# The seven late batches of x in L1's attention: rounded on a seven-step schedule, in place, and read back from DRAM

## The chip, the cores and the metric

The kernel runs on one core of one Trainium2 chip. The metric is the device time of one execution in microseconds. The core's engines are TensorE (PE, with its weight loads as PEld), VectorE (DVE), ScalarE (ACT), GpSimd (POOL) and SyncE (SP), which here only issues DMAs.

## The reference

The model takes x of 16 batches x 128 tokens x 256 and a context of the same shape through four layers, each `x = x + tanh(g) * attention(layernorm(x), ctx)` and then `x = x + tanh(g) * ffn(layernorm(x))`. The change lies in the attention of layer 1 (`_L1_xattn_ref`), cut to what matters:

```python
def _div_clamp_fp8(x, scale):
    y = jnp.clip(x / scale, -448, 448)
    y = y.astype(bfloat16)
    return fp8_e4m3_roundtrip(y)

ln_out = _ln(hidden_states, ln_w, ln_b)
q  = lin(ln_out, wq,  q_in_scale)     # each lin: _div_clamp_fp8(ln_out, its scale), then a matmul
k  = lin(ln_out, wk,  k_in_scale)
v  = lin(ln_out, wv,  v_in_scale)
qx = lin(ln_out, wqx, qx_in_scale)
q, k, qx = _ln per head (128 wide)
core = _gqa(q, k, v)                  # 16 heads, 8 groups
xout = _gqa(qx, _ln(kx), vx)          # kx, vx from the context, not rounded
catq = _div_clamp_fp8(concat(core, xout), proj_smooth)
return einsum(catq, wproj)
```

So the layer-normed x of each batch is needed in four versions, each scaled by its own vector and rounded to fp8. The rounding is done in bf16 with five operations on DVE (`round_fp8`).

## The kernel before, in words

Layer 1's attention (`l1_attention`) takes the 16 batches twice, once for each half of the eight head groups: Q = 32 passes q, each of J = 4 head groups, so N = 128 units n = 4q + j. Odd j are the cross-attention halves (they project the context too, L1525). The work is a software pipeline over steps s = 0 .. N + 21, which every engine walks through in the same order, each doing its own part of units at different depths:

- PE, in a step: `project(s-13)` (L1519, opens the step; the cross units L1525 too), `turn_x` for a late batch, `score(s-16)` (L1534), `values(s-18)` (L1543), `out_project(s-20)` (L1556), `turn_heads(s-15)` (L1567) and last `turn_probs(s-17)` (L1575), which waits for POOL's normalised probabilities.
- POOL, in a step: `statistics(s-14)` (L1832 to L1842: six small operations, of which the first waits for DVE's sum of squares L1756), the probabilities (L1876), the rounded output `l_cat` (L1883), then for a late batch `affine` (L1851, two operations), and in every step with s % 4 == 1 `put_cx_low` (L1858). All of it stands in one queue, in that order.
- DVE, in a step: smooth (L1736), sum of squares (L1756), the norm of the heads (L1767, both inputs in SBUF), row sums, maximum (L1778), five roundings of the output, and for s % 4 == 0 the addition to x (L1789).
- ACT, in a step: exponent (L1609), copies from PSUM (L1616, L1623), squares (L1630), the conversion of rounded x to fp32r for the matmuls (`put_xq`, L1665, `l_xq<-l_xs`), heads (L1637, L1638).

The rounded, four-fold x of a batch is 128 x 1024 bf16 (256 KB). For the batches 0 to 8 (AHEAD = 9) it is made earlier, beside the MoE layer of L0, and stored in DRAM (`saved`). The batches 9 to 15, called late, are made in the pipeline itself, during the first 16 passes: batch b in the steps from 4b on. Counted from s = 4b: +1 DVE normalises x (`norm_x`, L1772); +2 PE transposes it (`turn_x`) and ACT copies it out (`put_xb`); +3 ACT makes version 0 and POOL version 2 (`affine`); +4 ACT version 1, POOL version 3; +5, +6, +7, +7, +8 DVE does the parts 0, 1, 2, 3, 4 of `round_fp8` (L1244, L1246, L1248, L1250, L1251). Part 4 writes `XS` (`l_xs`), from which ACT reads one step later; SP also stores it to `saved` for the second 16 passes. SP fetches `XS` from DRAM for the other passes, at s = 4q + 5 for pass q, four steps before `put_xq` reads it.

The order of all work is written out by hand in the functions `sync`, `tensor`, `scalar`, `vector` and `gpsimd`; engines wait for each other through semaphores, and each engine runs its queue in order.

## Time and profile before

| what | value |
|---|---|
| median of 3 runs | 2357.87 us (2356.43 to 2365.08) |
| profiled execution, its own time | 2360.09 us |
| its span, first to last instruction | 2358.3 us |
| PE busy | 2120.3 us, 90% |
| DVE busy | 1872.0 us, 79% |
| ACT busy | 1358.7 us, 58% |
| POOL busy | 1246.9 us, 53% |
| mean granted TensorE clock | 0.956 |
| DMA | 82.35 MB, 10.1% of 16 engines' time in the main queue |

The span is shorter than the execution's own time by 1.8 us, which lies before the first and after the last instruction. The steps of L1's attention run from about 444 to 1260 us. In the views that follow, a row of a timeline is one instruction or a run of equal ones on one engine: its start from the span's start, its length, and in brackets how long the engine had been idle and who ended that. A busy POOL or DVE instruction may include time in which it was held up after it had started: the same operation on the same shape then shows two lengths.

### The profile page before, as it was taken

The numbers are of one execution on the slowest core, as the hardware profiler recorded it, in microseconds if no ns is written. First come the engines' busy times: TensorE is split into PE (matmuls) and PEld (weight loads), VectorE is DVE, ScalarE is ACT, GpSimd is POOL, SyncE is SP. The second block draws the span as 40 slices with busy tenths as digits, with TensorE's granted clock in tenths as the row PEclk, the third lists the DMA queues.
The fourth block names the chain that finished last, engine by engine and source line by source line (L and its number), as shares of the span: only waits on it lengthen the run. The fifth ranks groups of instructions, "written<-read, shape, count | busy, mean of one in ns | idle before, by whom it ended". The sixth has DMA issues, their size and how long they took to land.

```text
span 2358.3 us, 42828 instructions
## 1 busy us (share of the span) xinstructions
PE 2120.3 (90%) x14158; PEld 1760.8 (75%) x14158; DVE 1872.0 (79%) x3851; ACT 1358.7 (58%) x3426; POOL 1246.9 (53%) x1752
## 2 busy tenths in 40 slices
PE   5969999699999988999997899998899998659997
PEld 2348888589888877888886788886788887336665
DVE  5865687699999988999998677776578886777886
ACT  2213354688888877888885433333354455767773
POOL 4913343288999978999996211110344454741222
PEclk9979999799999999999999999998799999878998
DMA  4211121310000020000000300001000000010001
GB/s 133 83 38 65 43 86 54 125 35 18 11 17 15 23 81 19 17 15 19 17 6 13 119 21 27 21 21 59 8 8 8 8 6 1 1 50 20 24 24 37
DMA packets 39930, 82.35 MB, mean 35 GB/s; under 512 B 6048, under 2 KB 25824, under 8 KB 35776
## 3 DMA queue, kind: packets, MB, share of 16 engines
q1 hardware_dynamic: 39712, 79.60, 10.1%
q8 instruction: 117, 1.92, 0.3%
q14 instruction: 101, 0.83, 0.1%
HBM read 67.00 MB, written 12.58 MB: 34 GB/s over the span
## 4 chain that ended last, share of the span: by engine, by line
PE 61%; DVE 15%; POOL 11%; issue 6%; ACT 6%; DMA 1%; DVEq 0%; SPq 0%; ACTq 0%; POOLq 0%
PE bank L896 6%; PE bank L499 6%; PE bank L1519 5%; PE bank L309 4%; PE bank L1534 4%; PE bank L1556 3%; PE bank L912 3%; PE bank L1543 3%; PE bank L518 3%; PE bank L2620 2%; PE bank L1525 2%; POOL l_tiny L1834 2%; PE bank L1567 2%; PE bank L2008 2%; PE bank L1575 2%
## 5 line engine op out<-in xcount | busy, mean ns | idle before, releaser
L1519 PE MATMUL bank<-l_wr,l_xq 128*128 128x256 f32 (+1 forms) x1024 | 215.4, 354 | 17.7 <-ACT l_xq L1665 14.0
L896 PE MATMUL bank<-m_xr,m_wgr 128*128 128x512 f32 x864 | 211.8, 394 | 1.6 <-DVE m_xr L1015 1.6
L1519 PEld LDWEIGHTS bank<-l_wr,l_xq 128*128 128x128 f32 x1024 | 159.9, 193 | 36.4 <-issue 19.3
L896 PEld LDWEIGHTS bank<-m_xr,m_wgr 128*128 128x128 f32 x864 | 159.1, 190 | 32.4 <-issue 2.2
L1834 POOL TENSOR_TENSOR l_tiny<-l_tiny,l_minus_half 128x6 f32<-128x6 f32 x128 | 176.4, 1378 | 10.7
L1637 ACT ACTIVATE xn_T<-bank,l_head_b,l_head_w 128x512 f32<-128x512 f32 x128 | 99.7, 779 | 128.1 <-PE bank L1567 128.1
L1556 PE MATMUL bank<-l_wpr,l_cat 128*128 128x256 f32 x1024 | 168.3, 307 | 1.9 <-POOL l_cat L1883 1.9
L814 POOL TENSOR_TENSOR m_wgr<-m_wg,m_wgr 128x512 fp32r<-128x512 f32 x18 | 23.2, 1291 | 262.3 <-ACT m_wgr L803 262.3
L1534 PE MATMUL bank<-xn_T 128*128 128x128 f32 x1024 | 141.0, 281 | 18.9 <-ACT xn_T L1609 17.3
L1534 PEld LDWEIGHTS bank<-xn_T 128*128 128x128 f32 x1024 | 129.2, 193 | 32.6 <-issue 25.3
L1222 POOL TENSOR_SCALAR l_stage<-l_stage,l_means,l_full_scale 128x128 f32<-128x128 f32 x80 | 69.2, 878 | 159.3 <-DVE l_means L1209 159.3
L1883 POOL TENSOR_TENSOR l_cat<-l_yo,l_eo 128x512 fp32r<-128x512 bf16 x128 | 149.8, 1170 | 5.2 <-DVE l_yo L1250 5.2
L1623 ACT COPY l_raw<-bank 128x512 f32<-128x512 f32 x256 | 140.3, 612 | 20.6 <-PE bank L1525 14.5
L1767 DVE TENSOR_TENSOR l_raw<-l_raw,l_tiny 128x768 f32<-128x768 f32 x128 | 151.4, 1183 | 0.1
L1556 PEld LDWEIGHTS bank<-l_wpr,l_cat 128*128 128x128 f32 x1024 | 141.5, 192 | 9.2 <-POOL l_cat L1883 2.3
L2215 POOL TENSOR_TENSOR l_pr<-l_pr,l_rowsum 128x512 f32<-128x512 f32 x64 | 67.4, 1053 | 152.4 <-DVE l_rowsum L2183 152.4
L1609 ACT ACTIVATE xn_T<-bank,l_negmax 128x128 f32<-128x128 f32 x512 | 146.1, 378 | 2.6 <-DVE l_negmax L1778 2.6
L499 PE MATMUL bank<-m_xr,m_high 128*128 128x512 f32 x448 | 147.1, 410 | 0.0
L1876 POOL TENSOR_TENSOR xn_T<-xn_T,l_rowsum 128x512 f32<-128x512 f32 x128 | 136.8, 1069 | 11.9 <-DVE l_rowsum L1809 11.8
L2667 ACT ACTIVATE l_pr<-bank,l_negmax 128x256 f32<-128x256 f32 x256 | 118.0, 474 | 38.4 <-DVE l_negmax L2699 38.4
L1543 PE MATMUL bank<-xn_T,l_raw 128*128 128x256 f32 x512 | 134.3, 385 | 1.5 <-DVE l_yo L1736 0.8
L951 ACT ACTIVATE m_sg<-bank 128x512 f32<-128x512 f32 x72 | 43.1, 598 | 154.1 <-PE bank L896 154.1
(358 smaller groups left out, 6292.7 us busy)
## 6 DMA issues: line engine op xcount, KB each, us to landing
l_stage<-in_l_w SPq DMA_DIRECT2D x8, 1024.0 KB, 4.9
l_xs<-l_saved SPq DMA_DIRECT2D x25, 256.0 KB, 2.6
l_centred<-l_stage SPq DMA_DIRECT2D x6, 1024.0 KB, 4.1
l_stage<-l_centred SPq DMA_DIRECT2D x6, 1024.0 KB, 4.8
m_unsplit<-in_m_w SPq DMA_DIRECT2D x14, 384.0 KB, 3.2
m_wg<-in_m_gu SPq DMA_DIRECT2D x18, 256.0 KB, 2.6
x_norm<-in_ctxT_b SPq DMA_DIRECT2D x32, 128.0 KB, 2.0
l_stage<-in_l_wp SPq DMA_DIRECT2D x4, 1024.0 KB, 4.9
```

The source lines that it names most:

```text
L499: r = e.matmul(banks[2 * (n % 2) + half][:, :], weight[a][:, t, at:at + P], XR[:, b, k, g % 2, :], start=k == 0 and m == 0, stop=k == KT - ...
L896: r = e.matmul(banks[2 * (n % 2) + half][:, :], WGR[:, u % 2, a, k, half, :], XR[:, b, k, cols], start=k == 0 and m == 0, stop=k == KT - 1 ...
L1519: r = e.matmul(to, XQ[:, q % 2, v, k, :], WR[:, j, part, k, h0 * P:h1 * P], start=k == 0 and part == 0, stop=k == KT - 1 and part == 1)
L1534: r = e.matmul(pscore[:, h * P:(h + 1) * P], QT[:, n % 2, h, :], QT[:, n % 2, 4 + h // 2, :], start=True, stop=True)
L1543: r = e.matmul(pout[:, 2 * x * P:2 * (x + 1) * P], RAW[:, n % 6, 6 + x, :], tok(PT[:, n % 2, 2 * x:2 * x + 2, :]), start=True, stop=True)
L1556: r = e.matmul(pacc[:, 0:D], CAT[:, n % 2, h, :], WPR[:, j, part, h, :], start=j == 0 and h == 0 and part == 0, stop=j == J - 1 and h == 3 ...
L1609: r = e.activation(PR[:, n % 2, h, :], pscore[:, h * P:(h + 1) * P], ACT.Exp, bias=negmax[:, n % 2, h:h + 1])
L1623: r = e.copy(tok(RAW[:, n % 6, 4 * m:4 * m + 4, :]), bank[:, :])
L1767: e.tensor_tensor(heads(n), heads(n), bc(tiny[:, n % 2, 3, :], 2, P), ALU.mult).then_inc(s_norm.sem, 1)
L1834: pool_own.did(e.tensor_tensor(r0, var, minus_half[:, :], ALU.pow))
L1876: e.tensor_tensor(PR[:, n % 2, :, :], PR[:, n % 2, :, :], bc(rowsum[:, n % 2, :], 2, P), ALU.mult).then_inc(s_prob.sem, 1)
L1883: e.tensor_tensor(tok(CAT[:, n % 2, :, :]), YO[:, n % 2, :], EO[:, :], ALU.subtract).then_inc(s_cat.sem, 1)
```

## The change

The seven late batches are now tied to a table, `LATE_AT = {14 + 7 * i: 9 + i}`: batch 9 starts at step 14, batch 10 at 21, and so on to batch 15 at 56. All its parts keep their distance from the start (+1 norm, +2 transpose, +3 and +4 the scaled versions, +5 to +8 the rounding), so that one batch's last part (+8) now falls in the step of the next batch's norm (+1) and otherwise no two batches overlap. The last rounding part writes in place (`YQ`) instead of to `XS`; SP stores `YQ` to `saved` at +9; and all 32 passes fetch `XS` from DRAM at s = 4q + 5, so that the late batches too come back by a DMA. Each affine of batch b now waits for the store of batch b - 2. There are seven fetches more, and no other instruction is added or removed.

```diff
--- before.py
+++ after.py
@@ -1360,6 +1360,7 @@
 
 
 
+
             ready, weights = staged
             in_mul, in_add, head_w, head_b, smooth, coef, minus_half, s_ready, saved = ready
             order, at, w_loaded, s_cent, load_weights, unsplit, unsplit_out = weights
@@ -1395,6 +1396,7 @@
             YO = sb(scratch, "l1_yo", [P, 2, 4 * P], BF16)
             EO = sb(scratch, "l1_eo", [P, 4 * P], BF16)
             LATE = B - AHEAD
+            LATE_AT = {14 + 7 * i: AHEAD + i for i in range(LATE)}
             s_whi = signals("weights_high", G)
             s_wlo = signals("weights_low", G)
             m0_ends = ends
@@ -1437,7 +1439,7 @@
             s_affine_p = signals("l1_affine_p", LATE)
             s_xs = signals("x_rounded", LATE)
             s_store = Slots(signals, "l1_x_stored", LATE, 16, 2)
-            s_fetch = Slots(signals, "l1_x_fetched", B + AHEAD, 16, 2)
+            s_fetch = Slots(signals, "l1_x_fetched", Q, 16, 2)
             s_xq = signals("l1_xq", NS * Q)
             s_ctx = Slots(signals, "ctx_loaded", Q, 16, 2)
             s_cxh = signals("x_high", Q)
@@ -1481,20 +1483,16 @@
                         q = s // J - 1
                         e.wait_ge(*s_cx(q - 1))
                         e.dma_start(CN[:, q % 2, :, :], A["ctxT_b"][q % B]).then_inc(s_ctx.of(q), 16)
-                    if s % J == 1 and AHEAD <= s // J - 2 < B:
-                        b = s // J - 2
+                    if s - 9 in LATE_AT:
+                        b = LATE_AT[s - 9]
                         e.wait_ge(*s_xs(b - AHEAD + 1))
-                        e.dma_start(saved[b], XS[:, b % 2, :]).then_inc(s_store.of(b - AHEAD), 16)
+                        e.dma_start(saved[b], YQ[:, b % 2, :]).then_inc(s_store.of(b - AHEAD), 16)
                     q = s // J - 1
-                    if s % J == 1 and 2 <= q < AHEAD:
+                    if s % J == 1 and 2 <= q < Q:
+                        if AHEAD <= q < B:
+                            e.wait_ge(*s_store(q - AHEAD + 1))
                         e.wait_ge(*s_xq(NS * (q - 1)))
-                        e.dma_start(XS[:, q % 2, :], saved[q]).then_inc(s_fetch.of(q), 16)
-                    if s % J == 1 and B <= q < Q:
-                        if q - B >= AHEAD:
-                            e.wait_ge(*s_store(q - B - AHEAD + 1))
-                        e.wait_ge(*s_store(LATE - 1 + (LATE + q - AHEAD) % 2))
-                        e.wait_ge(*s_xq(NS * (q - 1)))
-                        e.dma_start(XS[:, q % 2, :], saved[q - B]).then_inc(s_fetch.of(q - LATE), 16)
+                        e.dma_start(XS[:, q % 2, :], saved[q % B]).then_inc(s_fetch.of(q), 16)
 
             def tok(ap):
                 return ap.rearrange("p n t -> p (n t)")
@@ -1588,8 +1586,8 @@
                 for s in range(END):
                     if 0 <= s - 13 < N:
                         project(e, s - 13)
-                    if s % J == 2 and AHEAD <= s // J < B:
-                        turn_x(e, s // J, s - 15)
+                    if s - 2 in LATE_AT:
+                        turn_x(e, LATE_AT[s - 2], s - 15)
                     if 0 <= s - 16 < N:
                         score(e, s - 16)
                     if 0 <= s - 18 < N:
@@ -1597,7 +1595,7 @@
                     if 0 <= s - 20 < N:
                         out_project(e, s - 20)
                     if 0 <= s - 15 < N:
-                        turn_heads(e, s - 15, s // J - AHEAD + 1 if s % J == 2 and AHEAD <= s // J < B else 0)
+                        turn_heads(e, s - 15, LATE_AT[s - 2] - AHEAD + 1 if s - 2 in LATE_AT else 0)
                     if 0 <= s - 17 < N:
                         turn_probs(e, s - 17)
 
@@ -1650,7 +1648,7 @@
 
                 e.wait_ge(*s_xb(b - AHEAD + 1))
                 if b >= AHEAD + 2:
-                    e.wait_ge(*s_xs(b - AHEAD - 1))
+                    e.wait_ge(*s_store(b - AHEAD - 1))
                 for k in range(KT):
                     to = (v * KT + k) * P
                     r = e.activation(YQ[:, b % 2, to:to + P], XB[:, k, :], ACT.Identity, bias=in_add[:, v, k:k + 1],
@@ -1659,7 +1657,7 @@
                     r.then_inc(s_affine_a.sem, 1)
 
             def put_xq(e, q, v):
-                e.wait_ge(*(s_xs(q - AHEAD + 1) if AHEAD <= q < B else s_fetch(q + 1 if q < B else q - LATE + 1)))
+                e.wait_ge(*s_fetch(q + 1))
                 if q >= 2:
                     e.wait_ge(*s_proj(J * (q - 1)))
                 e.copy(tok(XQ[:, q % 2, v, :, :]), XS[:, q % 2, v * KT * P:(v + 1) * KT * P]).then_inc(s_xq.sem, 1)
@@ -1690,15 +1688,14 @@
                         exponent(e, s - 17)
                     if 0 <= s - 18 < N:
                         put_probs(e, s - 18)
-                    if r == 2 and AHEAD <= b < B:
-                        put_xb(e, b)
+                    if s - 2 in LATE_AT:
+                        put_xb(e, LATE_AT[s - 2])
                     if 0 <= s - 13 < N:
                         raw(e, s - 13)
                         square(e, s - 13)
-                    if r == 3 and AHEAD <= b < B:
-                        affine_here(e, b, 0)
-                    if r == 0 and AHEAD < b <= B:
-                        affine_here(e, b - 1, 1)
+                    for v in range(2):
+                        if s - 3 - v in LATE_AT:
+                            affine_here(e, LATE_AT[s - 3 - v], v)
                     if 13 <= s and (s - 9) // NS < Q:
                         put_xq(e, (s - 9) // NS, (s - 9) % NS)
                     if r == 1 and 3 <= b < Q + 2:
@@ -1718,11 +1715,7 @@
                     e.wait_ge(*s_affine_p(b - AHEAD + 1))
                 else:
                     e.wait_ge(*quantised[b])
-                if part == 4:
-                    if b >= AHEAD + 2:
-                        e.wait_ge(*s_store(b - AHEAD - 1))
-                    e.wait_ge(*s_xq(NS * (b - 1)))
-                r = round_fp8(e, part, YQ[:, b % 2, :], EQ[:, :], XS[:, b % 2, :])
+                r = round_fp8(e, part, YQ[:, b % 2, :], EQ[:, :], YQ[:, b % 2, :])
                 if part == 4:
                     r.then_inc(s_xs.sem, 1)
                 else:
@@ -1782,7 +1775,7 @@
                 begin(e, ends)
                 e.wait_ge(*s_ready(1))
                 for s in range(END):
-                    n, r = s - 21, s % J
+                    n = s - 21
                     if 0 <= n < N and n % J == J - 1:
                         q, b = n // J, n // J % B
                         e.wait_ge(*s_outp(n + 1))
@@ -1809,16 +1802,17 @@
                         e.reciprocal(rowsum[:, (s - 17) % 2, :], rowsum[:, (s - 17) % 2, :]).then_inc(s_inv.sem, 1)
                     if out:
                         round_out(e, s - 19, 2)
-                    if AHEAD <= (s - 5) // J < B:
-                        quantise_x(e, (s - 5) // J, ((s - 5) % J, 4)[(s - 5) % J == 3])
+                    for after, part in ((5, 0), (6, 1), (7, 2), (8, 4)):
+                        if s - after in LATE_AT:
+                            quantise_x(e, LATE_AT[s - after], part)
                     if out:
                         round_out(e, s - 19, 3)
                     if 0 <= s - 16 < N:
                         maximum(e, s - 16)
-                    if r == 3 and AHEAD <= (s - 7) // J < B:
-                        quantise_x(e, (s - 7) // J, 3)
-                    if r == 1 and AHEAD <= s // J < B:
-                        norm_x(e, s // J)
+                    if s - 7 in LATE_AT:
+                        quantise_x(e, LATE_AT[s - 7], 3)
+                    if s - 1 in LATE_AT:
+                        norm_x(e, LATE_AT[s - 1])
                     if s in low_at:
                         fill_low(e, low_at[s])
                     if 14 <= s < 18:
@@ -1845,7 +1839,7 @@
 
                 e.wait_ge(*s_xb(b - AHEAD + 1))
                 if b >= AHEAD + 2:
-                    e.wait_ge(*s_xs(b - AHEAD - 1))
+                    e.wait_ge(*s_store(b - AHEAD - 1))
                 for k in range(KT):
                     to = (v * KT + k) * P
                     r = e.tensor_scalar(YQ[:, b % 2, to:to + P], XB[:, k, :], in_mul[:, v, k:k + 1], in_add[:, v, k:k + 1],
@@ -1881,10 +1875,9 @@
                         if n >= 2:
                             e.wait_ge(*s_outp(n - 1))
                         e.tensor_tensor(tok(CAT[:, n % 2, :, :]), YO[:, n % 2, :], EO[:, :], ALU.subtract).then_inc(s_cat.sem, 1)
-                    if r == 3 and AHEAD <= s // J < B:
-                        affine(e, s // J, 2)
-                    if r == 0 and AHEAD < s // J <= B:
-                        affine(e, s // J - 1, 3)
+                    for v in (2, 3):
+                        if s - 1 - v in LATE_AT:
+                            affine(e, LATE_AT[s - 1 - v], v)
                     if r == 1 and 3 <= s // J < Q + 2:
                         put_cx_low(e, s // J - 2)
                     if s in out_at and out_at[s] >= J:
```

**POOL.** The queue around one late batch's second affine. Before, step 44 (from its `l_cat`) to step 45; l_yq is the tile that is rounded, l_cxr the context's low part, l_tiny the statistics.

```order
L1883 TENSOR_TENSOR l_cat<-l_yo,l_eo 128x512
L1851 TENSOR_SCALAR l_yq<-xn_T,l_in_mul,l_in_add 128x128 x2
L1832 TENSOR_SCALAR l_tiny<-l_ssq 128x6
L1834 TENSOR_TENSOR l_tiny<-l_tiny,l_minus_half 128x6
L1836 TENSOR_TENSOR l_tiny<-l_tiny 128x6
L1838 TENSOR_TENSOR l_tiny<-l_tiny 128x6
L1840 TENSOR_SCALAR l_tiny<-l_tiny 128x6
L1842 TENSOR_TENSOR l_tiny<-l_tiny 128x6
L1876 TENSOR_TENSOR xn_T<-xn_T,l_rowsum 128x512
L1883 TENSOR_TENSOR l_cat<-l_yo,l_eo 128x512
L1858 TENSOR_TENSOR l_cxr<-x_norm,l_cxr 128x256
```

In the change, the same for batch 10, step 25 to 26 (its line numbers are lower by 6).

```order
L1877 TENSOR_TENSOR l_cat<-l_yo,l_eo 128x512
L1845 TENSOR_SCALAR l_yq<-xn_T,l_in_mul,l_in_add 128x128 x2
L1852 TENSOR_TENSOR l_cxr<-x_norm,l_cxr 128x256
L1826 TENSOR_SCALAR l_tiny<-l_ssq 128x6
L1828 TENSOR_TENSOR l_tiny<-l_tiny,l_minus_half 128x6
L1830 TENSOR_TENSOR l_tiny<-l_tiny 128x6
L1832 TENSOR_TENSOR l_tiny<-l_tiny 128x6
L1834 TENSOR_SCALAR l_tiny<-l_tiny 128x6
L1836 TENSOR_TENSOR l_tiny<-l_tiny 128x6
L1870 TENSOR_TENSOR xn_T<-xn_T,l_rowsum 128x512
L1877 TENSOR_TENSOR l_cat<-l_yo,l_eo 128x512
```

Before, the second affine always stands one step ahead of the `l_cxr` operation; here both stand in one step, and the statistics of the next unit behind both.

**DVE.** Before, a step with s % 4 == 1: part 0 of one batch (l_yq) and the norm of the next batch (L1772).

```order
L1762 TENSOR_REDUCE l_rowsum<-xn_T 128x4
L1246 TENSOR_SCALAR l_eo<-l_yo 128x512
L1809 RECIPROCAL l_rowsum<-l_rowsum 128x4
L1248 TENSOR_SCALAR l_eo<-l_eo 128x512
L1244 TENSOR_SCALAR l_yq<-l_yq 128x1024
L1250 TENSOR_TENSOR l_yo<-l_yo,l_eo 128x512
L1778 TENSOR_REDUCE l_negmax<-bank 128x4
L1772 TENSOR_SCALAR xn_T<-x_resident,ln_mean,ln_rstd 128x256
L1736 TENSOR_TENSOR l_yo<-bank,l_smooth 128x512
```

In the change, the step in which two batches meet, once in seven steps (its line numbers are lower by 7, L1251 apart).

```order
L1755 TENSOR_REDUCE l_rowsum<-xn_T 128x4
L1246 TENSOR_SCALAR l_eo<-l_yo 128x512
L1802 RECIPROCAL l_rowsum<-l_rowsum 128x4
L1248 TENSOR_SCALAR l_eo<-l_eo 128x512
L1251 TENSOR_TENSOR l_yq<-l_yq,l_eq 128x1024
L1250 TENSOR_TENSOR l_yo<-l_yo,l_eo 128x512
L1771 TENSOR_REDUCE l_negmax<-bank 128x4
L1765 TENSOR_SCALAR xn_T<-x_resident,ln_mean,ln_rstd 128x256
L1729 TENSOR_TENSOR l_yo<-bank,l_smooth 128x512
```

The norm now meets part 4, which writes l_yq and not l_xs, in place of part 0.

**SP.** Before, the DMAs around the first stores of late batches.

```order
L1483 DMA x_norm<-in_ctxT_b 128x256 x2
L1487 DMA l_saved<-l_xs 128x1024
L1483 DMA x_norm<-in_ctxT_b 128x256
L1487 DMA l_saved<-l_xs 128x1024
L1483 DMA x_norm<-in_ctxT_b 128x256
L1487 DMA l_saved<-l_xs 128x1024
```

In the change, a stretch at the same depth of the queue.

```order
L1485 DMA x_norm<-in_ctxT_b 128x256
L1489 DMA l_saved<-l_yq 128x1024
L1495 DMA l_xs<-l_saved 128x1024
L1485 DMA x_norm<-in_ctxT_b 128x256
L1495 DMA l_xs<-l_saved 128x1024
L1485 DMA x_norm<-in_ctxT_b 128x256
L1489 DMA l_saved<-l_yq 128x1024
L1495 DMA l_xs<-l_saved 128x1024
L1485 DMA x_norm<-in_ctxT_b 128x256
```

Fetches of l_xs from DRAM, which were absent for seven passes, go on, and a store stands between them once in seven steps.

## Rows read from the trace of the kernel before

**Rows 1.** The page's head: busy us of each engine, share of the span, instructions

```profile
PE 2120.3 (90%) x14158; PEld 1760.8 (75%) x14158; DVE 1872.0 (79%) x3851; ACT 1358.7 (58%) x3426; POOL 1246.9 (53%) x1752
```

**Rows 2.** Windows of the first mixture of L1: stretch, length, busy us (instructions) PE, PEld, DVE, ACT, POOL, clock

```profile
494.79:592.54 97.75, 97.41 (x658) 87.94 (x657) 90.47 (x165) 79.72 (x181) 88.00 (x132) 1.00 0.06 18
592.54:800.07 207.53, 197.23 (x1328) 176.76 (x1327) 198.08 (x371) 172.92 (x396) 191.65 (x294) 1.00 0.05 17
933.58:1253.04 319.46, 318.98 (x2134) 286.12 (x2133) 299.26 (x547) 258.36 (x583) 289.13 (x430) 1.00 0.05 14
```

**Rows 3.** Chain of waits, shares by line, of 513 to 538 us

```profile
by line: PE bank L1519 22.4%; PE bank L1543 16.5%; PE bank L1534 16.0%; PE bank L1556 15.2%; PE bank L1525 11.0%; PE bank L1567 10.5%; PE bank L1575 9.5%
```

**Rows 4.** Chain of waits, shares by line, of 592.54 to 800.07 us

```profile
by line: POOL l_tiny L1834 19.5%; POOL l_cat L1883 16.8%; issue 13.4%; POOL xn_T L1876 11.1%; POOL l_yq L1851 10.7%; POOL l_tiny L1832 6.8%; POOL l_cxr L1858 5.1%; POOL l_tiny L1836 3.8%; POOL l_tiny L1838 3.5%; POOL l_tiny L1840 3.0%; POOL
```

**Rows 5.** Timeline of PE: start, us, engine, line, operation [idle before <-releaser]

```profile
607.37 1.17 PE L1519 MATMUL bank<-l_wr,l_xq 128*128 128x512 f32 x4
...
613.43 0.66 PE L1575 MATMUL bank<-ident,xn_T 128*128 128x128 f32 x4 [0.17 <-POOL xn_T L1876]
613.85 2.12 PE L1519 MATMUL bank<-l_wr,l_xq 128*128 128x512 f32 x12
...
620.19 0.66 PE L1575 MATMUL bank<-ident,xn_T 128*128 128x128 f32 x4 [0.86 <-POOL xn_T L1876]
620.60 1.17 PE L1519 MATMUL bank<-l_wr,l_xq 128*128 128x512 f32 x4
...
640.18 2.12 PE L1519 MATMUL bank<-l_wr,l_xq 128*128 128x512 f32 x12
...
646.76 1.17 PE L1519 MATMUL bank<-l_wr,l_xq 128*128 128x512 f32 x4
...
653.17 2.11 PE L1519 MATMUL bank<-l_wr,l_xq 128*128 128x512 f32 x12
...
659.70 1.17 PE L1519 MATMUL bank<-l_wr,l_xq 128*128 128x512 f32 x4
...
666.34 1.88 PE L1519 MATMUL bank<-l_wr,l_xq 128*128 128x512 f32 x10
```

**Rows 6.** Timeline of POOL and L1767, 510 to 529 us, at the pace of PE

```profile
510.60 1.04 POOL L1832 TENSOR_SCALAR l_tiny<-l_ssq 128x6 f32<-128x6 f32 x1 [0.67 <-DVE l_ssq L1756]
...
516.37 0.95 DVE L1767 TENSOR_TENSOR l_raw<-l_raw,l_tiny 128x768 f32<-128x768 f32 x1
516.38 0.99 POOL L1832 TENSOR_SCALAR l_tiny<-l_ssq 128x6 f32<-128x6 f32 x1
...
523.14 0.79 POOL L1832 TENSOR_SCALAR l_tiny<-l_ssq 128x6 f32<-128x6 f32 x1
...
528.66 0.99 POOL L1832 TENSOR_SCALAR l_tiny<-l_ssq 128x6 f32<-128x6 f32 x1
```

**Rows 7.** Timeline of POOL, 606 to 662 us, among the late batches

```profile
614.63 1.60 POOL L1851 TENSOR_SCALAR l_yq<-xn_T,l_in_mul,l_in_add 128x128 bf16<-128x128 f32 x2
...
621.26 1.46 POOL L1858 TENSOR_TENSOR l_cxr<-x_norm,l_cxr 128x256 fp32r<-128x256 f32 x1
...
648.97 0.20 POOL L1832 TENSOR_SCALAR l_tiny<-l_ssq 128x6 f32<-128x6 f32 x1
...
653.90 0.99 POOL L1832 TENSOR_SCALAR l_tiny<-l_ssq 128x6 f32<-128x6 f32 x1
```

**Rows 8.** Timeline of all engines, 464 to 482 us, where the pipeline fills

```profile
473.44 0.78 ACT L1637 ACTIVATE xn_T<-bank,l_head_b,l_head_w 128x512 f32<-128x512 f32 x1 [0.76 <-PE bank L1567]
...
474.94 0.84 POOL L1832 TENSOR_SCALAR l_tiny<-l_ssq 128x6 f32<-128x6 f32 x1 [0.35 <-DVE l_ssq L1756]
...
480.01 0.20 POOL L1832 TENSOR_SCALAR l_tiny<-l_ssq 128x6 f32<-128x6 f32 x1 [0.71 <-DVE l_ssq L1756]
```

**Rows 9.** The tile l_xs: ns min/median/max, first and last start; landing of its DMAs

```profile
L1251 DVE TENSOR_TENSOR l_xs<-l_yq,l_eq x7: 684/712/716, 636.3 to 793.1; 128x1024 bf16<-128x1024 bf16 x7
...
DMA to landing us min/median/max: 2.0/2.6/5.5
```

## The prediction

> **What bounds the kernel now.** I first read the page's head and then only the stretch that the change can reach. PE is busy for 90% of the span [rows 1], so the question is where its other 10% goes. The windows split the first sixteen passes of L1's attention [rows 2]. In the 16 steps 21 to 36, without late batches, a step takes 97.75 / 16 = 6.11 us and PE is busy all but 0.34 us of the window. In the 32 steps 37 to 68, among the late batches, the window is 207.53 us, and 32 x 6.11 would be 195.5: the late batches cost 12.0 us together, 1.7 us each. That is all there is to win. Second, the chain of waits tells who sets the pace. Among steps without late batches it runs through PE alone [rows 3]; among the late ones it runs through POOL's queue, l_tiny, l_cat, xn_T and l_yq [rows 4]. So POOL is the engine to argue about, not DVE, although DVE is the busier (198.08 of 207.53 us [rows 2]).
>
> **Where the 12.0 us arise.** PE's L1519 opens each step, so differences of its starts are step lengths [rows 5]. Batch 9's first affines (L1851) fall at the ends of steps 39 and 40, when nothing has disturbed the pipeline. The steps behind them, 40 and 41, take 6.48 (607.37 to 613.85) and 6.75 us (613.85 to 620.60), which is 0.37 + 0.64 = 1.0 us over 6.11. PE waits 0.17 and 0.86 us there for POOL's probabilities, again 1.0 together. In the steady state the steps 45, 46, 47 and 48 take 6.58, 6.41, 6.53 and 6.64 us, 1.72 over 4 x 6.11. Steps 48 and 45, behind the affines, give 0.53 + 0.47 = 1.0 of it; steps 46 and 47, with the transpose and the rounding, 0.30 + 0.42 = 0.72.
>
> Why 0.17 and 0.86, where the affine pair takes 1.60 us [rows 7]? In an undisturbed step POOL's first operation, L1832, lasts 0.99 us in one step and 0.79 in another [rows 6], and 0.20 where POOL is late [rows 7]: it is held up, and a late POOL gets that time back. So POOL has 0.79 us to spare before a step with s % 4 = 1 or 3 (516.38 and 528.66 [rows 6]) and 0.59 before s % 4 = 2 (523.14, behind the l_cxr operation). Before s % 4 = 0 it has 0.67 idle and 0.84 held up, 1.51 [rows 6]. Taking 1.65 for an affine pair (1.60 [rows 7] and the wait around it), the loss is 0.14 in front of a step with s % 4 = 0, 0.86 in front of 1 or 3, and 1.06 in front of 2. The first two are what PE's waits show (0.17 and 0.86). The third is not in the trace: its bounds are 0.1, the best place, and 1.65, no relief at all, and I take 1.06 because it comes out of the rule that gave the other two.
>
> POOL's hold-up in L1832 lasts as long as DVE's L1767 beside it, 516.37 to 517.32 us [rows 6], and L1767 stands in every step, late batch or not. The Trainium skill (SBUF — State Buffer, "Who interferes with whom") says that a VectorE instruction with two SBUF inputs and a GpSimd instruction that reads SBUF exclude each other for their whole length. By that rule spreading the rounding frees nothing, since L1767 stands in every step. If only the rounding operations held the affines up, some 0.7 us would come free at each of 14 affine pairs, an estimate of 10 us. The rows at hand bear out the first.
>
> **The change part by part.**
> - *Affine pairs.* Before, they fell at s % 4 = 3 and 0, in front of steps 0 and 1: 1.0 us a batch. Now they stand in steps 17 and 18, 24 and 25, 31 and 32, 38 and 39, 45 and 46, 52 and 53, 59 and 60. In front of the steps 25 and 26: 0.86 + 1.06 = 1.9. 32 and 33: 0.14 + 0.86 = 1.0. 39 and 40: 0.86 + 0.14 = 1.0. 46 and 47: 1.9. 53 and 54: 1.9. 60 and 61: 1.0. Together 8.7 us. The order shows the bad case: the second affine and the l_cxr operation in one step.
> - *Batch 9*, now in steps 15 to 22, where the pipeline fills. POOL still has gaps of 0.35 and 0.71 us before steps 18 and 19, and ACT one of 0.76 in step 17 [rows 8]; ACT gets `put_xb` and two affine pairs. The trace has no such case: at least 0, if the gaps take all of it, at most two whole POOL pairs, 3.3 us. I take 1.2, two pairs less those gaps and hold-ups.
> - *Transpose and rounding.* The same operations, with the same distances from each other. The steady 0.72 us per batch arises in two steps, and in the change at least as many steps have such work: 7 x 0.72 = 5.0 us. At the least this is 0, if each now fits in DVE's idle time. The step in which part 4 meets the norm gets 0.71 [rows 9] and some 0.4 us; step 47 had as much (parts 2 and 3) and lost 0.42.
> - *In place* costs nothing: L1250, a rounding part that writes its own input, is in the kernel already.
> - *Seven fetches and later stores.* A transfer lands 2.6 us after its issue, 5.5 at worst [rows 9], and has four steps, 24 us. The last store is released in step 64 and the fetch of pass 15 waits for it in step 65; two transfers, 11 us at worst, against the need in step 69. No engine waits. On SP the store stands in front of a context load that has four steps to spare. The wait of each affine for a store of five steps ago is met.
> - *Removed:* DVE's waits for the tile `XS`, all met long before. 0.
>
> Sum of the new cost: 8.7 + 1.2 + 5.0 = 14.9 us against 12.0, so 2.9 us more. Against the profiled execution (2360.09 us, span 2358.3) this gives 2363.0; the median of the runs is 2.2 us lower, 2357.87, and the forecast is made against it: **2360.8 us**. A measurement of this kernel can tell 0.5% from no change, 11.8 us, so this is no change.
>
> **The rivals.**
> - *Capacity decides, not places.* In undisturbed steps DVE idles 97.75 - 90.47 = 7.3 us in 16 steps, 0.46 a step, POOL 9.75, 0.61 a step [rows 2]. Late batches add to busy time 198.08 - 32 x 5.65 = 17 us on DVE, 2.4 a batch, and 191.65 - 32 x 5.50 = 15.7 on POOL, 2.2 a batch. Four steps have 1.8 and 2.4 us of idle time for that, seven 3.2 and 4.3: at seven steps both fit. For it speaks a bare POOL step of 4.93 us, 648.97 to 653.90 [rows 7], and that the chain lies on POOL throughout. Against it: batch 9's affines hit a pipeline that was not full, and PE lost 1.0 us at once; PE, at 100% around them, never gives it back. If only 0.42 a batch is left (step 47's loss), 2.9 us remain of 12.0: 2357.9 - 9.1 = 2348.8 us. Everything gone would be 2345.9.
> - *POOL piles up (slower).* Where both affines stand in front of steps 1, 2 or 3 and beside the l_cxr operation, no hold-up is recovered: each pair costs its 1.65, and l_cxr its long form, 1.46 us [rows 7] against 0.79. That is 3.3 + 0.67 + 0.72 = 4.7 us in four batches (9, 10, 13, 14), and 1.7 in three, 23.9 in all, 11.9 more: 2369.8 us. It counts as slower from 3.4 us for an average batch on. Against it: the rule of recovered hold-ups fits both places seen.
> - *The way through DRAM is late.* If the fetched x came after its step, ACT would wait for l_xq seven times, by a landing each, 7 x 2.6 = 18 us: 2376. Only a transfer ten times as long as those seen would do it.
>
> **How the numbers follow.** Forecast 0.62, capacity 0.26, pile-up 0.10, DRAM 0.02. The forecast's own bounds: the unseen place (three times -0.9 or +0.6), batch 9 (-1.2 or +2.1) and the rounding term (down to 3) give 2355 to 2365. Half of the capacity case reaches below 2350, most of the pile-up case lies above 2366. Range 2350 to 2366. Faster by over 0.5% (below 2346.1) needs the capacity case with nearly nothing left, 0.03. Slower (above 2369.7): the pile-up's upper part and DRAM, 0.06. No change: 0.91.
>
> **What would show it.** Right: the chain of waits in steps 15 to 64 lies on PE for long parts and on POOL around the affines; PE waits 0.1 to 0.2 us for xn_T in front of steps 32, 40 and 60 and 0.8 to 1.1 in front of 25, 26, 46, 47, 53 and 54; steps in which no late work stands take 6.1 us; l_xq is never waited for; the steps 15 to 68 together lose about 15 us over 6.11 each. Wrong: waits of PE for POOL are below 0.5 us in front of 26, 46 and 54, or L1767 grows shorter (then capacity decided); or POOL stays late over several steps behind an affine (pile-up).

## The result, and the profile after

| what | before | after |
|---|---|---|
| median of the runs of this comparison | 2358.47 us (2356.34 to 2365.08, 14 runs) | 2368.39 us (2351.76 to 2466.98, 14 runs) |
| ratio, 95% interval | | 1.0036 [1.0024, 1.0049] |
| profiled execution, its own time | 2360.09 us | 2372.85 us |
| its span | 2358.3 us | 2371.1 us |
| mean granted TensorE clock | 0.956 | 0.950 |
| DMA moved | 82.35 MB | 84.18 MB |

One run of the changed kernel, at 2466.98 us, was a slow one (mean granted clock 0.825) and is left out of the ratio; without it the median of the other 13 is 2366.72 us. The median of all 14 lies 7.6 us above the forecast of 2360.8 us and above the range, which ended at 2366; that of the 13 is 5.9 above the forecast and 0.7 above the range. The ratio is 0.36% above 1, its interval lies wholly above 1, and it is below the 0.5% that the prediction called no change.

The page's head of the changed kernel answers to [rows 1]. PE is busy 11 us longer with the same 14158 matmuls: it did the same work more slowly.

```profile
PE 2131.4 (90%) x14158; PEld 1770.5 (75%) x14158; DVE 1873.0 (79%) x3851; ACT 1359.2 (57%) x3426; POOL 1248.4 (53%) x1752
```

The windows view of the changed kernel (columns as in [rows 2]): the same 48 steps that [rows 2] cover in two windows, then the same part of the second mixture.

```profile
496.69:801.72 305.03, 293.12 (x1982) 264.38 (x1981) 288.62 (x532) 251.34 (x570) 277.31 (x419) 1.00 0.08 23
932.02:1253.00 320.98, 320.42 (x2146) 287.62 (x2145) 300.11 (x548) 259.20 (x583) 290.44 (x433) 1.00 0.05 14
```

These 48 steps take 305.03 us where they took 97.75 + 207.53 = 305.28 [rows 2]. So the place that the change reaches is not where the time went. PE's timeline of the changed kernel shows that its waits moved to the steps that the prediction named; their sum is near the forecast, the single waits are not all. These are waits of L1573 in the steps 25 and 26, behind one affine pair, then 32 and 33, 39 and 40, 46 and 47, 53 and 54 (in brackets the idle time and who ended it):

```profile
524.01 0.66 PE L1573 MATMUL bank<-ident,xn_T 128*128 128x128 f32 x4 [0.24 <-POOL xn_T L1870]
...
531.59 0.66 PE L1573 MATMUL bank<-ident,xn_T 128*128 128x128 f32 x4 [1.25 <-POOL xn_T L1870]
...
569.02 0.65 PE L1573 MATMUL bank<-ident,xn_T 128*128 128x128 f32 x4 [0.35 <-POOL xn_T L1870]
...
575.61 0.66 PE L1573 MATMUL bank<-ident,xn_T 128*128 128x128 f32 x4 [0.70 <-POOL xn_T L1870]
...
613.38 0.66 PE L1573 MATMUL bank<-ident,xn_T 128*128 128x128 f32 x4 [0.53 <-POOL xn_T L1870]
...
620.33 0.66 PE L1573 MATMUL bank<-ident,xn_T 128*128 128x128 f32 x4 [0.62 <-POOL xn_T L1870]
...
658.43 0.66 PE L1573 MATMUL bank<-ident,xn_T 128*128 128x128 f32 x4 [1.01 <-POOL xn_T L1870]
...
665.30 0.66 PE L1573 MATMUL bank<-ident,xn_T 128*128 128x128 f32 x4 [0.98 <-POOL xn_T L1870]
...
702.73 0.66 PE L1573 MATMUL bank<-ident,xn_T 128*128 128x128 f32 x4 [0.24 <-POOL xn_T L1870]
...
710.30 0.66 PE L1573 MATMUL bank<-ident,xn_T 128*128 128x128 f32 x4 [1.24 <-POOL xn_T L1870]
```

POOL's timeline between the first two shows the case that the trace of before did not have: the affine pair and the l_cxr operation in one step, with the next statistics shrunk to 0.20 us behind them, which is what a late POOL looks like in [rows 7].

```profile
525.12 1.59 POOL L1845 TENSOR_SCALAR l_yq<-xn_T,l_in_mul,l_in_add 128x128 bf16<-128x128 f32 x2
526.68 0.73 POOL L1852 TENSOR_TENSOR l_cxr<-x_norm,l_cxr 128x256 fp32r<-128x256 f32 x1
527.49 0.20 POOL L1826 TENSOR_SCALAR l_tiny<-l_ssq 128x6 f32<-128x6 f32 x1
```

The tile l_xs, now fetched for all 32 passes, is never waited for in the steady state. Its landings take at most 5.1 us, where before they took at most 5.5 [rows 9]. The one wait behind it, PE's 14.0 us for the first l_xq, stands at the start of the pipeline, and the kernel before has it too.

```profile
L1663 ACT CAST l_xq<-l_xs x128: 386/389/400, 443.4 to 1233.9; 128x256 fp32r<-128x256 bf16 x128
...
  PE bank L1517: 14.0, 1
...
DMA to landing us min/median/max: 2.4/2.6/5.1
```

Where then are the 12.8 us between the two spans? Matching PE's instructions one to one shows the distance between the two executions: +0.3 us at the pipeline's first step (444 us), +1.8 at step 69 (796.47 against 798.30), -1.6 at 913 us, -0.1 at PE's first matmul of L3's attention (2118.82 against 2118.68), and +12.4 some 50 us later, where it stays. All the excess arises at the start of L3's attention, 1300 us after the changed part. The windows of the changed kernel, counted from that first matmul:

```profile
2118.68:2138.68 20.00, 15.25 (x71) 10.92 (x72) 9.59 (x18) 11.96 (x44) 4.63 (x8) 0.50 0.10 27
2138.68:2148.68 10.00, 10.00 (x66) 6.99 (x65) 5.05 (x12) 4.75 (x19) 0.00 (x0) 0.50 0.03 7
2148.68:2158.68 10.00, 10.00 (x67) 6.99 (x66) 5.79 (x14) 4.75 (x19) 2.42 (x4) 0.50 0.07 21
2158.68:2168.68 10.00, 10.00 (x67) 6.99 (x66) 5.05 (x12) 4.75 (x18) 0.00 (x0) 0.50 0.02 3
2168.68:2178.68 10.00, 9.39 (x114) 6.62 (x112) 7.51 (x20) 7.60 (x28) 2.41 (x4) 0.94 0.09 27
```

The column PEclk reads 0.50, the level of 1.2 GHz, for 50 us behind that matmul. Behind the first 20 us PE is busy all the time and does 66 or 67 matmuls in 10 us, where it does 114 in the last window, at 0.94. The record of the granted clock has one low stretch from 2098.13 us, 71.68 us long; before, it began at 2098.88 and was 40.96 us long.

### The profile page after: what moved, and what is told of

Its sections match the earlier page's. It is cut to its first block, busy times and chain, and to the rows that moved or that the text cites. A ratio compares the mean times of both kernels' runs of the same rounds, so it can differ in the third digit from the quotient of the medians.

```text
span 2371.1 us, 42819 instructions
## 1 busy us (share of the span) xinstructions
PE 2131.4 (90%) x14158; PEld 1770.5 (75%) x14158; DVE 1873.0 (79%) x3851; ACT 1359.2 (57%) x3426; POOL 1248.4 (53%) x1752
## 2 busy tenths in 40 slices
DMA packets 40938, 84.18 MB, mean 36 GB/s; under 512 B 6160, under 2 KB 25936, under 8 KB 36784
## 4 chain that ended last, share of the span: by engine, by line
PE 60%; DVE 16%; POOL 10%; issue 7%; ACT 6%; DMA 1%; DVEq 0%; SPq 0%; ACTq 0%; POOLq 0%
PE bank L896 6%; PE bank L499 6%; PE bank L1517 4%; PE bank L309 4%; PE bank L912 3%; PE bank L1532 3%; PE bank L1554 3%; PE bank L1541 3%; PE bank L2613 3%; PE bank L518 3%; POOL l_tiny L1828 2%; PE bank L2001 2%; PE bank L1523 2%; PE bank L2601 2%; PE bank L1565 2%
## 5 line engine op out<-in xcount | busy, mean ns | idle before, releaser
L1517 PE MATMUL bank<-l_wr,l_xq 128*128 128x256 f32 (+1 forms) x1024 | 215.1, 353 | 18.6 <-ACT l_xq L1663 14.0
L1517 PEld LDWEIGHTS bank<-l_wr,l_xq 128*128 128x128 f32 x1024 | 160.0, 193 | 37.0 <-issue 19.9
L1828 POOL TENSOR_TENSOR l_tiny<-l_tiny,l_minus_half 128x6 f32<-128x6 f32 x128 | 178.4, 1393 | 10.7
L1877 POOL TENSOR_TENSOR l_cat<-l_yo,l_eo 128x512 fp32r<-128x512 bf16 x128 | 150.8, 1178 | 4.5 <-DVE l_yo L1250 3.1
L1760 DVE TENSOR_TENSOR l_raw<-l_raw,l_tiny 128x768 f32<-128x768 f32 x128 | 149.4, 1167 | 0.0
L1870 POOL TENSOR_TENSOR xn_T<-xn_T,l_rowsum 128x512 f32<-128x512 f32 x128 | 134.5, 1051 | 12.3 <-DVE l_rowsum L1802 12.3
```

Source lines behind the costliest of these rows:

```text
L1517: r = e.matmul(to, XQ[:, q % 2, v, k, :], WR[:, j, part, k, h0 * P:h1 * P], start=k == 0 and part == 0, stop=k == KT - 1 and part == 1)
L1760: e.tensor_tensor(heads(n), heads(n), bc(tiny[:, n % 2, 3, :], 2, P), ALU.mult).then_inc(s_norm.sem, 1)
L1828: pool_own.did(e.tensor_tensor(r0, var, minus_half[:, :], ALU.pow))
L1870: e.tensor_tensor(PR[:, n % 2, :, :], PR[:, n % 2, :, :], bc(rowsum[:, n % 2, :], 2, P), ALU.mult).then_inc(s_prob.sem, 1)
L1877: e.tensor_tensor(tok(CAT[:, n % 2, :, :]), YO[:, n % 2, :], EO[:, :], ALU.subtract).then_inc(s_cat.sem, 1)
```

## The experiments

There were eighteen runs more, eight of them of a kernel that had run already, each beside executions of the kernel before on the same chip. A run is several executions, of which one is profiled. Besides the median I give how many executions lie above 2362 us, and call these long and the others short. Of the kernel before, over all comparisons and once more as a kernel of its own, 20 of 153 do.

**The two kernels again.**

> The kernel before, unchanged, for a second profile. Theory A (the schedule's own cost is about 2 us, and most of the 10 us come from where TensorE's granted clock rises at the start of L3's attention): about 2358 us, with the clock rising some 21 us after PE's first matmul of L3 attention (L2608), as in the first profile (2118.8 to 2140). Theory B (the L1 schedule itself costs the 10 us, and the clock in L3 is the same for both kernels over many executions): about 2358 us, but the place where the clock rises in L3 moves from profile to profile, by tens of microseconds.

Measured: 2357.74 us (2354.43 to 2359.82), ratio 0.9999 [0.9990, 1.0008], none of 10 above 2362. Windows of its profile, from its first matmul of L3's attention:

```profile
2116.56:2136.56 20.00, 15.25 (x71) 10.92 (x72) 9.60 (x18) 11.95 (x44) 4.62 (x8) 0.50 0.08 26
2136.56:2146.56 10.00, 9.91 (x117) 6.86 (x115) 7.43 (x19) 7.43 (x28) 1.85 (x3) 0.95 0.09 28
2146.56:2156.56 10.00, 9.59 (x119) 6.85 (x120) 8.69 (x20) 8.38 (x32) 0.72 (x3) 1.00 0.10 28
```

For 20 us nothing tells it from the changed kernel: 71 matmuls, 15.25 us busy. Then its clock is back.

> The changed kernel, unchanged, for a second profile and more times. Theory A: times scattered from 2351 to 2375 us, in steps that go with the mean granted clock; if this profile is one of the shorter executions, the rise in L3's attention comes about 21 us after its first matmul and not 51. In L1's attention the step starts are the same as in the first profile within 0.5 us. Theory B: L1's attention differs from profile to profile by as much as the whole time does.

Measured: 2362.51 us (2353.03 to 2370.34), ratio 1.0014 [0.9997, 1.0031], 6 of 12 above 2362. The profile caught a short execution, 2355.14 us, with a low stretch of 40.96 us. The same program scatters over 17 us, so a single profile says little of its median.

**The start of L3's attention, first attempts.** Five copies on DVE, their result unused, hold PE's first matmul back:

```diff
+            def hold(e):
+                begin(e, hold_ends)
+                for k in range(4):
+                    e.wait_ge(*dve_own.all())
+                    dve_own.did(e.tensor_copy(xn[:, 0, :], X[:, 0, :]))
+                e.wait_ge(*dve_own.all())
+                e.tensor_copy(xn[:, 1, :], X[:, 0, :]).then_inc(held.sem, 1)
+            stage(vector=hold)
+            ends = ends + [held(1)]
```

> The kernel before with five copies on DVE (about 1.5 us) in front of L3's attention, which nothing else needs. Theory A: the start of L3's attention moves by 1.5 us against the chip's clock decisions, so the rise can come one decision later: about 2358 + 1.5 + 12 = 2371 us if it does, 2359.5 if the place has no such edge within 1.5 us. Theory B: 2359.5 us.

Measured: 2359.13 us (2353.28 to 2362.19), 1.0001 [0.9993, 1.0010], 1 of 11 above 2362; the matmul came 2.2 us later and the clock rose 22.2 us behind it. The delay did not bring a long stretch, 44.37 us against 40.96: at that point this spoke against the place.

Unused transposes in PE's pause ahead of it:

```diff
             def tensor(e):
+                for n in range(44):
+                    e.transpose(pacc[1][:, 0:P], ident[:, :], ident[:, :])
                 begin(e, ends)
                 score(e, 0, 0)
```

> The kernel before with 44 transposes of the identity on PE into an unused bank, in PE's 12 us pause in front of L3's attention. They compute nothing that is used. Theory A (clock outcomes): PE enters L3's attention busy, the low clock ends sooner after its first matmul than 21 us, up to 9 us are gained: 2349 to 2356 us. Theory B: PE's pause has no part in it: 2358 us.

> The same 44 transposes in the changed kernel. Theory A: the long low stretch in L3's attention (71.7 us in the first profile) disappears, and what is left against the kernel before with the same transposes is the schedule's own 2 us and the other clock places: 2351 to 2358 us, with less scatter than the changed kernel's 22 us. Theory B: 10 us above before_warm.

Measured: 2358.06 us (2356.93 to 2366.45), 0.9996 [0.9985, 1.0008], for the kernel before; 2367.37 us (2351.75 to 2379.74), 1.0027 [1.0010, 1.0045], 8 of 12 above 2362, for the changed one. Both profiles have 10.24 and 23.89 us of low clock there in place of 41, and yet the medians did not fall: an expectation missed. For the short executions the profiles say why: what the transposes took away lay ahead of the first matmul, in the pause. Behind it the clock still rose only after 20.96 us (before_warm) and 22.52 us (after_warm), where before_again has 21.05. Where the long executions with transposes lose their time was not seen (below, look_c).

**What the schedule costs by itself.** Starts every eighth step, so that no two batches meet; and starts chosen such that every affine pair stands in front of steps with s % 4 = 0 and 1:

```diff
-            LATE_AT = {14 + 7 * i: AHEAD + i for i in range(LATE)}
+            LATE_AT = {8 + 8 * i: AHEAD + i for i in range(LATE)}                                     # after_eight
+            LATE_AT = {at: AHEAD + i for i, at in enumerate((12, 20, 28, 36, 40, 48, 56))}            # places
```

> The changed kernel with LATE_AT = {8 + 8 * i}: a batch in eight steps, the first one before the pipeline is full, every affine pair in front of steps with s % 4 = 0 and 1. Place rule: six batches cost 1.0 + 0.4 to 0.7 us and the first next to nothing, so the steps 13 to 68 lose 9 to 11 us over 6.11 each, about 4 us less than the change with seven. Capacity: they lose under 4 us. What the whole time does depends on the clock (theory A): 2345 to 2370 us.

> The changed kernel with LATE_AT starting at 12, 20, 28, 36, 40, 48, 56, so that all affine pairs fall in front of steps with s % 4 = 0 and 1, at spacings of eight and four steps. Place rule: waits of PE for xn_T of 0.15 and 0.86 us behind each pair and none of 1 us or more; section 2 us shorter than the changed kernel's, 1.6 us a batch. Capacity: spacings of eight lose nothing, the one of four 1.7.

Measured: 2367.87 us (2352.51 to 2378.95), 1.0042 [1.0015, 1.0069], 5 of 7 above 2362; and 2364.02 us (2352.95 to 2371.53), 1.0020 [1.0000, 1.0040], 6 of 10. Every batch of the first shows the same waits of PE. Timeline of PE of the kernel with starts every eighth step, and its L1517 eight steps apart (the last row is cut off by the end of the window):

```profile
579.87 1.17 PE L1517 MATMUL bank<-l_wr,l_xq 128*128 128x512 f32 x4
...
598.27 0.66 PE L1573 MATMUL bank<-ident,xn_T 128*128 128x128 f32 x4 [0.15 <-POOL xn_T L1870]
...
605.04 0.66 PE L1573 MATMUL bank<-ident,xn_T 128*128 128x128 f32 x4 [0.86 <-POOL xn_T L1870]
...
617.75 0.66 PE L1573 MATMUL bank<-ident,xn_T 128*128 128x128 f32 x4 [0.32 <-POOL xn_T L1870]
...
630.32 0.94 PE L1517 MATMUL bank<-l_wr,l_xq 128*128 128x512 f32 x3
```

Eight steps take 50.45 us against 8 x 6.11 = 48.9: a batch that is alone costs 1.57 us, where four-step batches cost 1.7. Spreading has next to nothing to give. The pair in front of steps with s % 4 = 0 and 1 costs 0.15 + 0.86, as the rule of the places says. The second kernel shows 0.15 and 0.86 behind its isolated pairs too. From step 13 to step 69 the first takes 348.2 us, where the changed kernel takes 351.6 to 353.7 in seven profiles, about the 4 us less that were expected; but its step 13 starts 7.5 us later (451.86 us against 444.35 in the kernel before), since batch 9 now stands ahead of it, and its step 69 starts at 800.04 us, no earlier than the 796.47 us of the kernel before. The second takes 352.6; the 2 us less expected of it are not seen.

**In place and back from DRAM, with the spacing of before:**

```diff
-            LATE_AT = {14 + 7 * i: AHEAD + i for i in range(LATE)}
+            LATE_AT = {32 + 4 * i: AHEAD + i for i in range(LATE)}
```

> One part of the change alone: in place and back through DRAM, but with the four-step spacing, LATE_AT = {32 + 4 * i}, every affine pair at the places that the kernel before had. Place rule: section as before, steps 33 to 68 lose 12 us, ratio 1.000 within 0.3%. If the DRAM way or the in-place write costs, l_xq is waited for or L1251 is longer, and the section loses more than 13 us.

> dram_four unchanged, for more times and a second profile. It had the section's time of the kernel before and yet 6 of 10 executions above 2362 us, where the kernel before had 5 of 35. If that holds: again about half above 2362. If it was chance of one session: one in seven. In a long execution's profile the low clock should last over 41 us at L3's start.

Measured: 2363.97 us (2350.89 to 2375.74), 1.0017 [0.9998, 1.0036], 6 of 10 above 2362; again 2368.66 us (2357.87 to 2380.51), 1.0038 [1.0017, 1.0060], 10 of 12. In both profiles PE keeps the pace of the kernel before within 0.3 us up to 809 us. So the whole loss of the change, or more, comes back with the late batches just as dense as they were (they start one pass earlier, at step 32): the seven-step table is not needed for it. Whether the table would cost without the way through DRAM was not tried.

**The transfers alone.** The kernel before with the seven passes' 256 KB fetched as well, into a tile that nothing reads:

```diff
+                    if s % J == 1 and AHEAD <= q < B:
+                        e.wait_ge(*s_xq(NS * (q - 1)))
+                        for m in range(2):
+                            k = 2 * (q - AHEAD) + m
+                            if k:
+                                e.wait_ge(*s_spare(k))
+                            e.dma_start(SPARE[:, :], saved[q - AHEAD][:, 4 * P * m:4 * P * (m + 1)]).then_inc(s_spare.sem, 16)
```

> The kernel before with DMAs added that nothing needs: in the passes 9 to 15, where it does not fetch, the same 256 KB a pass from DRAM (as two halves) into a spare tile. Theory C (the seven more transfers make the clock outcomes scatter, as in all five kernels that go through DRAM and are otherwise unlike): half of the executions above 2362 us, mean 2362 to 2365 us. Theory A alone (the clock outcomes depend on the L1 schedule's times): as the kernel before, one in seven above 2362 us, mean 2358 to 2359 us.

Measured: 2358.70 us (2356.17 to 2365.76), 0.9994 [0.9978, 1.0011], 1 of 12 above 2362. No cost of the transfers can be seen.

**POOL's part taken away.** All four scaled versions are made by ACT, at +3 to +6 from a batch's start, and the rounding follows at +7 to +10; the starts are 12 + 7i:

```diff
-                    for v in range(2):
+                    for v in range(4):
                         if s - 3 - v in LATE_AT:
                             affine_here(e, LATE_AT[s - 3 - v], v)
...
-                    for v in (2, 3):
-                        if s - 1 - v in LATE_AT:
-                            affine(e, LATE_AT[s - 1 - v], v)
```

> The changed kernel with the late batches' POOL part taken away from POOL: all four scaled versions are made by ACT, in the steps +3 to +6, the rounding is two steps later, and LATE_AT = {12 + 7 * i}. Place rule: POOL's affine pairs cost 1.0 to 1.9 us a batch because PE waits for POOL in that very step; without them the steps 15 to 68 lose some 0.6 us a batch, 4 us, 8 to 10 less than the changed kernel. Rival: DVE's rounding is what costs, then they lose as much as before, 12 us. Whole time by the place rule about 2352, with the clock's scatter around it.

Measured: **2352.25 us** (2349.43 to 2363.08, 12 runs), ratio 0.9974 [0.9962, 0.9986], faster than both kernels. From step 21 to step 69 (493.31 to 790.28 us) it takes 296.97 us, where before_again takes 305.01 (491.60 to 796.61) and 48 steps without late batches would take 293.3. PE's longest wait for POOL between 500 and 660 us, from its timeline:

```profile
505.70 0.66 PE L1573 MATMUL bank<-ident,xn_T 128*128 128x128 f32 x4 [0.43 <-POOL xn_T L1868]
```

Of the 12.0 us, 8 are gone once POOL's affines no longer stand in its queue ahead of the probabilities; from step 13 on it is 7.2, as the steps 13 to 20 take 0.8 us more. (The rounding two steps later and the earlier starts came with it; their share was not tried apart.)

**More profiles, to catch long executions.** So far nearly every profile was a short execution.

> The changed kernel once more for a third profile: the low clock at the start of L3's attention lasts 41 or 72 us, and the time goes with it, 2353 to 2362 or 2365 to 2375 us.

> The changed kernel unchanged, to get a profile of a long execution (about half its executions are above 2362 us, the profile is one execution). Theory A (the loss of long executions is a longer stretch at low TensorE clock at the start of L3's attention): if this profile's span is above 2361, the low stretch there is 51 us or longer, where short executions have 41; if below, it is 41 to 44. Theory B (the loss is spread over the clock's low stretches elsewhere): a long profile has 41 there and its loss at 840 to 910, 1260 to 1300 or 1625 to 1710. The section of L1 with the late batches costs 1.2 to 2 us over the kernel before in either case.

> The kernel with a late batch every fourth step as before, in place and back from DRAM, once more for a profile of a long execution (16 of its 22 executions were above 2362 us, but both profiles were short, 2356). Theory A: a profile above 2361 has 51 us or more of low clock at the start of L3's attention. Theory B: it has 41 to 44 there and loses 5 us or more in other stretches. Theory C (not the clock: the program itself is longer in these executions, through DRAM or the DMA queues): the mean clock is that of the short ones and the drift arises at full clock.

> The changed kernel with the unused transposes in TensorE's pause ahead of L3's attention, whose profile was a short execution (2350 us span, 24 us of low clock there) though 8 of 12 executions were above 2362. Theory A: in a long execution the low stretch there is 40 us or more in spite of the transposes. Theory B: it stays at 24 and the loss stands in other stretches; then the start of L3's attention isn't the only place.

> As look_b, the same kernel a further time: about two of three executions are long, so of the two looks at least one should be. Same expectations by theory.

Measured: after_look is a single execution, 2356.39 us. The others have medians of 2366.28, 2366.47, 2367.87 and 2367.83 us (4, 4, 8 and 4 executions), ratios 1.0034 to 1.0043, all clear of 1. The profiles have spans of 2354.6, 2364.2, 2365.9, 2353.4 and 2372.4 us, with low stretches there of 40.96, 51.20, 61.44, 10.24 + 23.89 and 81.92 us. The three long ones all lose at this place: against before_again 4.4, 8.1 and 16.4 us. Their distance to it is +4.0, +2.2 and -0.1 us at the first matmul. So look_a loses about as much ahead of this place: it is level with before_again at 835 us and 5.1 us behind at 925 us, with low stretches at 844, 858, 878 and 909 us. The first profile of the kernel before has the like there, and 3.9 us, so this is no mark of the change. Windows of look_d:

```profile
2116.45:2136.45 20.00, 15.26 (x71) 10.92 (x72) 9.60 (x18) 11.94 (x44) 4.61 (x8) 0.50 0.09 27
...
2166.45:2176.45 10.00, 10.00 (x66) 6.99 (x65) 5.79 (x14) 4.82 (x18) 2.40 (x4) 0.50 0.09 27
2176.45:2186.45 10.00, 9.91 (x117) 7.01 (x116) 7.44 (x20) 7.70 (x28) 1.52 (x3) 0.93 0.10 28
```

Theory C (the program itself is longer) is out: up to there look_d is level with before_again. Theory B, with 41 us at this place, is out for these three. The 1.2 to 2 us that L1's section was to cost in look_a are not there: its steps 13 to 69 take 352.8 us, those of before_again 353.2. look_c was a short execution, though 7 of its 8 runs were above 2362, so for the kernel with transposes the question stays open.

**What decides at this place.** The low stretch does not begin in PE's pause but ahead of it. In the kernel before it begins at 2098.88 us, when PE still works with short waits, and the pause follows at 2106.84 us:

```profile
2098.96 1.03 PE L2386 MATMUL bank<-identb,l2f_hq 128*128 128x128 bf16 x8 [1.94 <-ACT l2f_hq L2425]
...
2104.94 1.89 PE L2364 MATMUL bank<-l2f_w,l2f_hqT 128*128 128x256 bf16 x8 [1.10 <-ACT l2f_hqT L2407]
2118.82 2.20 PE L2608 MATMUL bank<-l_ck,l_xq 32*128 32x256 f32 x16 [11.98 <-DMA l_ck<-in_ctx]
```

The fifteen profiles so far of kernels without the transposes, lined up by the distance from the start of the low stretch to PE's first matmul of L3's attention:

| distance, us | clock rises behind the matmul | profiles |
|---|---|---|
| 18.83 | 22.1 us | after_again |
| 19.70, 19.91, 19.94, 19.97, 20.01 | 20.9 to 21.3 | act_affine, before_again, before, dram_four, after_look |
| 20.12, 20.20, 20.23 | 31.0 to 31.1 | extra_fetch, after_eight, look_a |
| 20.35, 20.35 | 41.1 | look_b, places |
| 20.54 | 51.1 | after |
| 20.57 | 61.4 | look_d |
| 22.12 | 22.2 | before_hold |
| 23.44 | 20.9 | dram_again |

What is lost behind the matmul goes with the rise and not with the kernel: against before_again 4.4 us where the clock rises at 31, 8.1 at 41, 12.6 at 51 and 16.4 at 61, and extra_fetch, a kernel before with transfers added, is among the rows at 31. The length of the pause, the obvious rival, does not order the rows: 12.16 us in after_again and 12.65 in dram_again go with 22.1 and 20.9, 11.89 in after_eight with 31.0. The kernel before stands 0.2 us short of the first long row. Two more kernels move that matmul alone: one copy on DVE in the kernel before, `range(0)` in place of `range(4)` in the diff of before_hold, and the five copies in the changed kernel.

> The kernel before with one unused copy on DVE between the layernorm and L3's attention, so that PE's first matmul there comes some 0.4 us later. Theory A: what decides is the distance from the start of the low-clock stretch to that matmul. In the 14 profiles it is 19.7 to 20.01 us where the clock rises 21 us behind the matmul, 20.12 to 20.23 where it rises 31 us behind, 20.35 where 41, 20.54 and 20.57 where 51 and 61, and 18.83 and 22.12 where 22. The kernel before stands at 19.9, just short of the edge; 0.4 us more make it 20.3 to 20.5: the profile's low stretch is 61 us or longer, its time 2364 to 2372, and more than half of the executions are above 2362 us where about one in six of the kernel before is. Theory D (long executions belong to the way through DRAM or the new schedule, the distance only goes along with them): the copy costs 0.4 us, median 2358.5 to 2360, stretch 41 to 44, at most one in five above 2362.

> The changed kernel with five such copies, which in the kernel before moved the matmul by 2.2 us, to a distance of 22.1 us and a rise 22 us behind it. Theory A: the distance is 22 to 22.8, or 25.5 with a stretch that begins earlier, and the clock rises 22 us behind the matmul in nearly all executions: although 2 us of work are added the median falls, to 2359 to 2363, where the changed kernel unchanged has 2362.5 to 2368.4, and at most one in four is above 2364. Theory D: the copies cost 2 us, median 2364 to 2370, spread as before.

Measured, before_nudge: **2372.38 us** (2360.25 to 2375.46, 9 runs), ratio 1.0041 [1.0022, 1.0060]. The times form two groups, four at 2360.25 to 2361.97 and five at 2372.38 to 2375.46. The profile is of the second. PE's timeline (the row is cut off by the end of the window), then the windows from its first matmul:

```profile
2117.76 1.61 PE L2621 MATMUL bank<-l_ck,l_xq 32*128 32x256 f32 x9 [12.67 <-DMA l_ck<-in_ctx]
```

```profile
2117.76:2137.76 20.00, 15.26 (x71) 10.94 (x72) 9.60 (x18) 11.94 (x44) 4.61 (x8) 0.50 0.09 25
2137.76:2147.76 10.00, 10.00 (x66) 6.98 (x65) 5.05 (x12) 4.74 (x19) 0.00 (x0) 0.50 0.03 5
...
2157.76:2167.76 10.00, 10.00 (x67) 6.98 (x66) 5.05 (x12) 4.74 (x19) 0.00 (x0) 0.50 0.01 2
2167.76:2177.76 10.00, 9.38 (x114) 6.62 (x112) 7.50 (x20) 7.57 (x28) 2.41 (x4) 0.94 0.09 28
```

PE's pause is 12.67 us where before_again has 12.02, the distance is 20.51 us, and the clock rises 51.2 us behind the matmul, as in the changed kernel's profile row for row. Up to 1971 us it keeps within 0.6 us of before_again, and at 2287 us it is 13.8 behind. **A copy of half a microsecond, in a kernel without a line of the change, costs what the change cost.** The mean granted clock, which every execution has, is 0.949 to 0.951 in the five long ones and 0.957 to 0.959 in the four short ones. That shows the place, and that neither the schedule nor the way through DRAM is needed for the loss. The added stage by itself is not the reason: before_hold has the same one with four copies more and no group of long executions. That the matmul's distance within the low stretch decides was forecast and came true in this profile; it is one profile.

Measured, after_hold: 2366.98 us (2358.45 to 2373.12, 12 runs), ratio 1.0032 [1.0017, 1.0046]. Its profile, 2358.45 us, is as expected (distance 22.29, rise 22.1 us behind), but six of the twelve executions took 2369.75 to 2373.12 us: the median did not fall, and this half of the expectation was missed. No profile exists of those six. Their mean granted clock, 0.951 to 0.955 where the other six have 0.957 to 0.961, puts their loss down to the clock too, but where in the span, and at which distance, isn't known. If they had the distance of 22.3, the rule of the distance would be wrong.

## Why the prediction was wrong

- **The place** (32 late steps cost 12.0 us, the affine pairs 8.7 of it after the change). The sum held, the rule not place by place. PE's waits sum to 1.49, 1.05, 1.15, 1.99, 1.48 and 1.36 us for the six pairs where 1.9, 1.0, 1.0, 1.9, 1.9 and 1.0 were forecast: 8.5 against 8.7. The first and the fifth came out 0.4 us cheaper, the last 0.4 us dearer. Behind s % 4 = 2, the place unseen before, PE waits 1.25, 1.01 and 1.24 us, forecast 1.06 each; but in the steps 25 and 53 it waits 0.24 us, forecast 0.86, and in step 40 0.62, forecast 0.14. These errors cancel in the sum, which is in part luck. The chain of waits was to lie on PE for long parts of the steps 15 to 64; from 475 to 760 us it lies mostly on POOL (L1828 16.1%, L1877 9.1%, L1870 8.8%), and of PE's lines only L1517 has a larger share, 3.8%.
- **Batch 9 in the ramp**, 1.2 us, was too dear. From L1517 of step 13 to that of step 21 the changed kernel takes 47.1 to 48.5 us in seven profiles (the one with copies and the two with transposes included), mean 48.0, the kernel before and its variants 46.9 to 48.4 in six, mean 48.0. No cost can be seen.
- **Transpose and rounding**, 5.0 us, was too dear as well. Steps 21 to 69 take 305.03 us against a base of 48 x 6.11 = 293.3, 11.7 in all; less 8.5, 3.2 are left.
- **The sum**, +2.9 us for this section, comes out at about nothing: 8.5 + 3.2 = 11.7, against 12.0 before. In the seven profiles steps 21 to 69 take 303.9 to 305.2 us, in the six of the kernel before and its variants 305.0 to 305.3. So what the forecast left out elsewhere is 2.9 us more than the 7.6 us by which the median missed it.
- **In place, the fetches, the waits for stores** cost nothing in this section, as forecast; extra_fetch shows it for the fetches.
- **The exclusion of DVE and POOL.** L1760, the norm of the heads, takes 1167 ns on average (1183 before), and PE's waits did not go. The Trainium skill (SBUF — State Buffer, "Who interferes with whom") was used to say that spreading the rounding frees nothing as long as that operation stands in every step. The outcome agrees: at eight steps a batch it still cost 1.57 us. No run here took L1760 away, so this does not prove the exclusion.
- **The step that failed** is the last of the working: "the median of the runs is 2.2 us lower, 2357.87, and the forecast is made against it". It carried the rest of the program over unchanged, a term put at nothing without a reason. In the profiled pair 12.6 of the 12.8 us between the spans arise at the start of L3's attention. In the changed kernel the low stretch there is 51.20 us in one and 71.68 in another of four profiles and 40.96 in two, and each further 10.24 us of it cost about 4.1 us (8.1 for two, 12.6 for three, 16.4 for four). No term and no rival of the prediction held it, and the windows that were read ended at 1253 us. The other executions fit by their mean clock, the only record of most of them: of the eleven above 2362 us that count in the ratio, ten have 0.950 to 0.955, where the profiled executions with 40.96 us have 0.956 to 0.962.
- **The rivals.** Capacity is refuted (after_eight: 1.57 us a batch remain where both engines had room). The pile-up on POOL would have shown several late steps behind one pair; pairs sum to 1.99 us at most, not 3.3 and more. DRAM is not late: l_xq is waited for only at the start. The measured time comes near the pile-up's 2369.8 us, by another cause.

What stays open: why the changed kernel (21 of 30 executions of it unchanged above 2362 us), and the one with in place and DRAM alone (24 of 30), arrive at the long distances more often than the kernel before (20 of 153). In the table a distance longer by 0.1 to 0.6 us is enough, and the profiles show no single place from which it comes. In act_affine, which goes through DRAM too, only 4 of 12 executions are more than 3 us above its median, so DRAM alone does not settle it. And the long executions of after_warm and after_hold weren't seen in a profile.

## What to carry to other kernels

Before a small edit is costed, look in the whole trace for pauses of PE behind which the clock comes back late, and ask how near they stand to an edge: here half a microsecond went with 12.6. Take several profiles of a kernel whose runs scatter before its time is explained. Where an engine's queue delays the one that sets the pace, moving work to an engine with room (7 to 8 us here) does what spreading it in the same queue does not.

## What the runs showed of the hardware

- In the long profiles the granted clock of PE stayed at 0.50, the level of 1.2 GHz, for 31 to 61 us behind the first matmul of a stage, and in the windows shown PE was busy for 10.00 of every 10 us from the 20th us on. The Trainium skill (TensorE: Matmul & The Clock Gate, "What's actually happening") has activity release the clock. These traces agree in part: the clock did come back while PE worked, but in look_d only after some 40 us in which PE did not pause. The 12 us pause was not what lowered the clock: it fell 8.0 us ahead of it in the kernel before, after 20 us in which PE had been busy for 11.95.
- The rises came 21, 31, 41, 51 and 61 us behind the matmul and not between, save for 22 at three other distances (18.83, 22.12, 22.29). From before_again to before_nudge, which differ by one copy, the distance is 0.60 us longer (19.91 to 20.51) and the rise went from 21.0 to 51.2 us.
- 44 unused transposes in the pause split the low stretch into 10.24 and 23.89 us, 7 us less: the clock was at 1.00 for 6.83 us from 2106.41 us on, 2.3 us after the first transpose. Behind the first matmul it rose no sooner (20.96 us against 21.05), and the median of the kernel before stayed (0.9996 [0.9985, 1.0008]).
